# Feature interaction in fp32: pairs transposed and weighed eight at a time in two shared PSUM banks, with the two steps two sets of scores apart

## What is computed

```
bilinear = einsum('bie,ied->bid', feature, weight)
out      = einsum('bid,bjd->bij', bilinear, feature)
```

## Time and profile before

| | |
|---|---|
| time, median of 3 runs | 1518.4 us (1517.48 to 1518.64) |
| the profiled execution | 1516.77 us, its span 1514.9 us |
| TensorE matmul busy | 1452.9 us, 96% |
| VectorE busy | 1167.2 us, 77% |
| ScalarE busy | 893.5 us, 59% |
| DMA traffic | 438.67 MB, mean 290 GB/s |

### The profile page before, as it was taken

How to read it: one execution, slowest core, us unless ns; L and a number is a source line. 1 busy time by engine, 2 the same in 40 slices (tenths; PEclk the granted TensorE clock), 3 DMA queues, 4 the chain that set the end, 5 groups by cost and what they waited for, 6 DMA issues and landing times.

```text
span 1514.9 us, 41346 instructions
## 1 busy us (share of the span) xinstructions
PE 1452.9 (96%) x16192; PEld 1206.3 (80%) x16192; DVE 1167.2 (77%) x2048; ACT 893.5 (59%) x1313; POOL 294.3 (19%) x518
## 2 busy tenths in 40 slices
PE   7999999999999999999999999999999999999965
PEld 6888887888788787888778888788787888878754
DVE  0578778788777778778787787877877777887897
ACT  5665665656656565665656656566665656656532
POOL 0112112121221212122121121221212111121222
PEclk9999999999999999999999999999999999999999
DMA  8799999999999999999999999999999999999898
GB/s 220 225 289 288 305 300 290 299 288 304 300 290 296 294 300 292 303 290 287 290 294 303 294 295 305 292 297 292 296 299 292 301 284 305 298 292 297 265 275 257
DMA packets 308574, 438.67 MB, mean 290 GB/s; under 512 B 56480, under 2 KB 255136, under 8 KB 308384
## 3 DMA queue, kind: packets, MB, share of 16 engines
q1 hardware_dynamic: 283808, 422.80, 87.1%
q0 software_dynamic: 24576, 13.24, 6.0%
HBM read 108.13 MB, written 327.68 MB: 288 GB/s over the span
## 4 chain that ended last, share of the span: by engine, by line
PE 83%; DVE 10%; DMA 3%; issue 3%; SPq 1%; ACT 0%; POOLq 0%
PE ps L225 43%; PE bp L209 24%; PE tp L193 14%; DVE staging L256 4%; DMA x<-feature_dram 3%; DVE win L305 3%; DVE win L312 2%; PE ps L209 1%; DVE win L313 1%; PE ps L193 1%; SPq L143 0%; SPq L138 0%; SPq L131 0%; ACT staging L256 0%; ACT bl L279 0%
## 5 line engine op out<-in xcount | busy, mean ns | idle before, releaser
L225 PE MATMUL ps<-win,bl 64*100 64x200 f32 x8192 | 831.7, 344 | 42.8 <-DVE win L313 39.6
L225 PEld LDWEIGHTS ps<-win,bl 64*100 64x100 f32 x8192 | 696.5, 207 | 134.3 <-issue 67.1
L256 DVE COPY staging<-ps 100x800 f32<-100x800 f32 x512 | 503.9, 984 | 252.2 <-PE ps L225 252.2
L256 ACT COPY staging<-ps 100x800 f32<-100x800 f32 x512 | 423.3, 827 | 251.9 <-PE ps L225 251.9
L176 POOL DMA_DIRECT2D out_dram<-staging x512 | 293.6, 573 | 1213.3 <-DVE staging L256 985.5
L209 PE MATMUL bp<-xt,w 64*64 64x128 f32 x6144 | 419.6, 276 | 0.0
L209 PEld LDWEIGHTS bp<-xt,w 64*64 64x64 f32 x6144 | 326.7, 133 | 65.2 <-issue 65.2
L279 ACT COPY bl<-bp 128x512 f32<-128x512 f32 x384 | 225.2, 586 | 178.0 <-PE bp L209 178.0
L269 ACT COPY xt<-tp 128x512 f32<-128x512 f32 x384 | 225.1, 586 | 171.4 <-PE tp L193 171.4
L305 DVE COPY win<-xt 128x400 f32<-128x400 f32 x512 | 272.9, 533 | 64.5 <-ACT xt L269 48.8
L193 PE MATMUL tp<-ident,x 128*128 128x128 f32 x1536 | 252.9, 287 | 7.9 <-DMA x<-feature_dram 7.6
(11 more groups left out here) (5 smaller groups left out, 0.6 us busy)
## 6 DMA issues: line engine op xcount, KB each, us to landing
out_dram<-staging SPq DMA_DIRECT2D x1024, 300.0 KB, 4.7
x<-feature_dram SPq DMA_DIRECT2D x400, 256.0 KB, 5.1
out_dram<-staging POOLq DMA_DIRECT2D x512, 25.0 KB, 4.6
w<-weight_dram SPq DMA_DIRECT2D x24, 128.0 KB, 3.9
w<-weight_dram SPq DMA_DIRECT2D x2, 64.0 KB, 3.3
```

The costliest lines, as they stand in the source:

```text
L225: last = nc.tensor.matmul(ps[s % TILES][0:FH, h, F * b:F * (b + 1)], rows_of_bl(n, R * k + PB * i + b)[64 * h:64 * h + 64], win[64 * h:64 ...
L256: copy(staging[:, slot, :, :, :].rearrange("p b h j -> p h b j"), ps[s % TILES][0:FH, :, 0:PB * F].rearrange("p h (b j) -> p h b j", j=F)) ...
```

## The change

- A group is now eight pairs (12 groups of eight and one of four, NG = 13), and its `x` comes in one transfer of 512 KB. XSLOTS stays 4, so the slots hold twice as much.
- T makes eight transposes, B sixteen matmuls. Both write into the same two banks, `made`, which take the place of `tp` and `bp`. So a T now also waits for the last B's copy (`bl_stored`), and B for T's copy, as before.
- T and B are no longer next to each other. The places are counted in sets: T of group u after set 4u + 4 + 2(u // 6), and B of it two sets later. B of group 0 comes after set 4, T of the next block's first group after set 62.
- A transpose writes its 128 columns in runs of four numbers, 16 numbers apart, so that the PSUM tile already has the layout of `xt`. Before, the transpose wrote 128 neighbouring numbers and ScalarE's copy read runs of four.
- ScalarE copies a group at once: 1024 numbers per partition in place of two copies of 512.
- Output slots go from 16 to 12, windows from 3 to 4. SyncE issues the load of a group right after the T that frees its slot, four groups ahead.

The diff, cut to its core:

```diff
--- before.py
+++ after.py
-    NG = FH // C
+    LINES = FH // C
+    GROUPS = [8] * (FH // 8) + [FH % 8]
+    NG = len(GROUPS)
...
-    OSLOTS = 16
-    WSLOTS = 3
-    WG = 2
+    OSLOTS = 12
+    WSLOTS = 4
...
-    weighed_at = {t * 7 // 6: t for t in range(NG)}
-    transposed_at = {k: t + 1 for k, t in weighed_at.items() if t + 1 < NG}
-    transposed_at[QUADS - 1] = NG
+    transposed_at = {4 * u + 4 + 2 * (u // 6): u for u in range(1, NG)}
+    weighed_at = {s + 2: u for s, u in transposed_at.items()}
+    weighed_at[4] = 0
+    transposed_at[SETS_B - 2] = NG
...
-        x = sbuf("x", [128, XSLOTS, 2 * C * E])
+        x = sbuf("x", [128, XSLOTS, 16 * E])
...
-        tp = ctx.enter_context(nc.psum_tensor("tp", [128, 512], F32))
-        bp = ctx.enter_context(nc.psum_tensor("bp", [128, 512], F32))
+        made = ctx.enter_context(nc.psum_tensor("made", [128, 2, 512], F32))
...
-        def transpose_tile(n, t):
-            return tp_first[t % 3] if n == 0 else tp[:]
-
-        def bilinear_tile(n, t):
-            return bp_first[t % 3] if n == 0 else bp[:]
+        def transpose_tile(n, u):
+
+            tile = ps[0] if n == 0 and u % 2 else made
+            cells = tile[:].rearrange("p l (k c r) -> p l k c r", c=C, r=R)
+            return cells[:, 0:GROUPS[u] // C]
+
+        def bilinear_tile(n, u):
+            return ps[1 + u % 2] if n == 0 else made
...
-            for t in range(NG + XSLOTS):
-                if t % WG == 0 and t < NG:
-                    load_w(t // WG)
-                load_x(t)
+            for u in range(NG + 1 + XSLOTS):
+                if u < NG:
+                    load_w(u)
+                load_x(u)
             for n in range(BLOCKS):
-                for k in range(QUADS):
-                    store(n * SETS_B + 2 * k)
-                    store(n * SETS_B + 2 * k + 1)
-                    if k in transposed_at:
-                        at = (n + 1) * NG + transposed_at[k] + XSLOTS - 1
+                for s in range(SETS_B):
+                    store(n * SETS_B + s)
+                    if s in transposed_at:
+                        at = (n + 1) * NG + transposed_at[s] + XSLOTS
...
             def transposes(at):
...
                 if n:
                     pe.wait_ge(xt_stored, at)
-                elif t >= 3:
-                    pe.wait_ge(xt_stored, t - 2)
-                for c in range(C):
-                    last = nc.tensor.transpose(transpose_tile(n, t)[:, NB * c:NB * (c + 1)],
+                    pe.wait_ge(bl_stored, at)
+                elif u >= 2:
+                    pe.wait_ge(xt_stored, u - 1)
+                for c in range(GROUPS[u]):
+                    last = nc.tensor.transpose(transpose_tile(n, u)[:, c // C, :, c % C, :],
                                                x[:, at % XSLOTS, 2 * E * c:2 * E * (c + 1)], ident[:])
...
-                for k in range(QUADS):
-                    scores(n, k, 0)
-                    scores(n, k, 1)
-                    if k in transposed_at and (n + 1) * NG + transposed_at[k] < BLOCKS * NG:
-                        transposes((n + 1) * NG + transposed_at[k])
-                    if k in weighed_at and n + 1 < BLOCKS:
-                        bilinear(n + 1, weighed_at[k])
+                for s in range(SETS_B):
+                    scores(n, s // 2, s % 2)
+                    if s in transposed_at and (n + 1) * NG + transposed_at[s] < BLOCKS * NG:
+                        transposes((n + 1) * NG + transposed_at[s])
+                    if s in weighed_at and n + 1 < BLOCKS:
+                        bilinear(n + 1, weighed_at[s])
...
-                nc.scalar.copy(group_of_xt(n, t),
-                               transpose_tile(n, t).rearrange("p (c k r) -> p k c r", c=C, r=R)
+                nc.scalar.copy(group_of_xt(n, u), transpose_tile(n, u).rearrange("p l k c r -> p k l (c r)")
                                ).then_inc(xt_stored, 1)
...
-                nc.scalar.copy(group_of_bl(n, t), bilinear_tile(n, t).rearrange(cells, c=C)
-                               ).then_inc(bl_stored, 1)
+                rows = bilinear_tile(n, u)[:].rearrange("p a c -> p (a c)")[:, 0:NB * GROUPS[u]]
+                nc.scalar.copy(group_of_bl(n, u), rows.rearrange(cells, b=NB)).then_inc(bl_stored, 1)
```

More of the change, by code:

```diff
@@ L36, in feature_interaction @@
     TILES = 3
-    OSLOTS = 16
-    WSLOTS = 3
-    WG = 2
+    OSLOTS = 12
+    WSLOTS = 4
     FA = FH // 16 * 16
-    assert 2 * E == 128 and B % NB == 0 and FH % C == 0 and NG <= QUADS and R == 2 * PB
-    assert PB * F <= 512 and C * NB == 512 and OSLOTS % 2 == 0 and (BLOCKS * SETS_B) % OSLOTS == 0
+    assert 2 * E == 128 and B % NB == 0 and FH % 8 == C and R == 2 * PB
+    assert PB * F <= 512 and OSLOTS % 2 == 0
     feature_v = feature.rearrange("b f e -> b (f e)")
@@ L46, in feature_interaction @@
     out_v = out.rearrange("b (m h) j -> m b (h j)", h=2)
-    weighed_at = {t * 7 // 6: t for t in range(NG)}
-    transposed_at = {k: t + 1 for k, t in weighed_at.items() if t + 1 < NG}
-    transposed_at[QUADS - 1] = NG
-    assert len(weighed_at) == NG and max(weighed_at) < QUADS - 2 and all(k >= t for k, t in weighed_at.items())
+    transposed_at = {4 * u + 4 + 2 * (u // 6): u for u in range(1, NG)}
+    weighed_at = {s + 2: u for s, u in transposed_at.items()}
+    weighed_at[4] = 0
+    transposed_at[SETS_B - 2] = NG
+    assert all(s >= 2 * min(2 * u + 1, LINES - 1) + 1 for s, u in weighed_at.items())
     ctx = ExitStack()
@@ L96, in feature_interaction, with line_of_xt, group_of_xt, group_of_bl @@
         block = ctx.enter_context(nc.Block())
-        def transpose_tile(n, t):
-            return tp_first[t % 3] if n == 0 else tp[:]
-        def bilinear_tile(n, t):
-            return bp_first[t % 3] if n == 0 else bp[:]
-        def group_of_xt(n, t):
-            return xt[:, t, :, :, :] if n % 2 == 0 else xt[:, :, t, :, :]
+        def transpose_tile(n, u):
[4 more added lines that the diff above has]
+            return ps[1 + u % 2] if n == 0 else made
+        def line_of_xt(n, t):
+            return xt[:, t, :, :, :] if n % 2 == 0 else xt[:, :, t, :, :]
+        def group_of_xt(n, u):
+            lines = slice(2 * u, 2 * u + GROUPS[u] // C)
+            if n % 2 == 0:
+                return xt[:, lines].rearrange("p l k c r -> p k l (c r)")
+            return xt[:, :, lines].rearrange("p k l c r -> p k l (c r)")
         def quad_of_xt(n, k):
-            return xt[:, 0:NG, k, :, :] if n % 2 == 0 else xt[:, k, 0:NG, :, :]
-        def group_of_bl(n, t):
+            return xt[:, 0:LINES, k, :, :] if n % 2 == 0 else xt[:, k, 0:LINES, :, :]
+        def group_of_bl(n, u):
             if n % 2 == 0:
-                return bl[:, C * t:C * (t + 1), :]
-            return bl[:, :, C * t:C * (t + 1)]
+                return bl[:, 8 * u:8 * u + GROUPS[u], :]
+            return bl[:, :, 8 * u:8 * u + GROUPS[u]]
         def rows_of_bl(n, b):
@@ L234, in _ @@
             transposes(1)
[L235 to L238, removed]
+            for u in range(NG):
+                bilinear(0, u)
+                if u + 2 < NG:
+                    transposes(u + 2)
             transposes(NG)
             for n in range(BLOCKS):
-                for k in range(QUADS):
-                    scores(n, k, 0)
-                    scores(n, k, 1)
-                    if k in transposed_at and (n + 1) * NG + transposed_at[k] < BLOCKS * NG:
-                        transposes((n + 1) * NG + transposed_at[k])
-                    if k in weighed_at and n + 1 < BLOCKS:
-                        bilinear(n + 1, weighed_at[k])
+                for s in range(SETS_B):
[4 more added lines that the diff above has]
+                        bilinear(n + 1, weighed_at[s])
         def stage(engine, copy, staged, s):
@@ L262, in store_xt @@
             def store_xt(at):
-                n, t = at // NG, at % NG
+                n, u = at // NG, at % NG
                 act.wait_ge(transposed, at + 1)
+                lines = GROUPS[u] // C
                 if n:
                     act.wait_ge(bilinear_done, n * NG)
-                    act.wait_ge(own_filled, (n - 1) * QUADS + t + 1)
-                nc.scalar.copy(group_of_xt(n, t),
-                               transpose_tile(n, t).rearrange("p (c k r) -> p k c r", c=C, r=R)
+                    act.wait_ge(own_filled, (n - 1) * QUADS + 2 * u + lines)
@@ L288, in _ @@
             store_xt(NG)
             for n in range(BLOCKS):
-                for k in range(QUADS):
-                    stage(act, nc.scalar.copy, staged_act, n * SETS_B + 2 * k)
-                    if k in transposed_at and (n + 1) * NG + transposed_at[k] < BLOCKS * NG:
-                        store_xt((n + 1) * NG + transposed_at[k])
-                    if k in weighed_at and n + 1 < BLOCKS:
-                        store_bl(n + 1, weighed_at[k])
+                for s in range(SETS_B):
+                    if s % 2 == 0:
```

(5 more changed lines are left out.)

53 lines of the change are left out of this document (26 added, 27 removed).

## The result

| | before | after |
|---|---|---|
| median | 1517.9 us (1515.8 to 1518.6, 4 runs) | 1465.1 us (1464.6 to 1466.7, 4 runs) |
| ratio, 95% interval | | 0.9656 [0.9639, 0.9673] |
| profiled execution | 1516.8 us | 1466.7 us |
| its span | 1514.9 us | 1464.8 us |
| the scores begin at | 51.55 us | 53.46 us |

The change makes the kernel 3.4% faster. The forecast was 1451 us with a range of 1436 to 1492. The two profiled executions lie 50.1 us apart and the medians 52.8 us. The sum had said 67.5.

The account below looks back on a forecast made before the run. TensorE's own list was taken to set the pace of the 15 mixed blocks. 53.1 + 10.5 + 2 + 1.9 = 67.5 us off 1516.8 gave 1449.3; with 1.6 us for the median, 1451 us, range 1436 to 1492.

Parts of the forecast that it names:

- Fewer bursts: TensorE, 15 mixed blocks: 12 fewer bursts each of T and B save 3.54 us a block, 53.1 us in all.
- New neighbours: TensorE: T now followed by scores and B preceded by them; extra price 0 to 0.12 us, taken as 0.
- The rival of 0.12 us: Scores behind a T are dearer by 0.12 us, 23 us over 15 blocks: 1474 us; chance 0.12.
- The shared banks: T and B wait for each other's ScalarE copy, 1.01 us for 1024 numbers, covered by two sets: cost nothing.
- late copies: Rival: ScalarE's two-bank copy takes 1.6 us or is queued, T and B wait some 0.1 us each: 1490 us; chance 0.04.
- The end of a block: VectorE's stall falls from 2.0 us to 1.2 (even) or up to 1.5 (odd): 0.7 us less a block, 10.5 in all.
- the ledger: Count of VectorE's copies from set 59's start: set 57's copy ended at -0.64, rounds end at 4.32, 6.61 and 8.90 us.
- Opening: Before the scores: 12 fewer bursts of each kind save 3.5 us, larger first transfers cost some; 2 us less taken.
- `x` transfers: Loads issued four groups ahead, some 24 us in place of 9, so the 1.9 us of waits for `x` go.
- The DMA rival: Mixed blocks ask for 308 GB/s; if the DMA engines give 300, a block takes 90.1 us: 1486 us; chance 0.10.
- The slower rival: Transposes writing PSUM in runs of four with gaps take 0.22 us, not 0.11: 165 us more, 1616 us; chance 0.09.
- The rule on changes of tiling mode: Skill's rule: TensorE pays 0.18 us per mode change, so eight pairs save 0.36, not 0.295 us: 12 us more, 1439 us.

Follow-up runs that it names:

- experiment 2: Kernel before, with T moved between the two sets of a quad, so one more burst of scores a round: 1599.9 us, ratio 1.052.
- Experiment 6: Changed kernel with the two-set gaps at groups 4, 8 and 12 in place of 6 and 12: 1453.2 us, ratio 0.9568 to the kernel before.
- experiment 1: Kernel before, but its transposes write runs of four numbers with gaps, as in the changed kernel: 1516.1 us, ratio 0.9982.
- experiment 4: Kernel before with four windows in place of three and 12 output slots in place of 16: 1517.5 us, ratio 1.0004.
- Experiment 12: Changed kernel loading only the first group's weights and using them in every group: 1459.7 us, ratio 0.9601 to the kernel before.
- experiment 3: Changed kernel with three windows in place of four: 1568.4 us, ratio 1.0322 to the kernel before.
- experiment 7: Changed kernel with ScalarE, not VectorE, staging sets 57, 61 and 1 of each block: 1459.1 us, ratio 0.9612 to the kernel before.
- experiment 9: Kernel of experiment 7 with 14 output slots in place of 12 and three `x` slots in place of four: 1462.7 us, ratio 0.964.
- experiment 8: Kernel of experiment 7, loading only half of each group's `x` from block 1 on, all computing kept: 1437.3 us, ratio 0.948.
- experiment 10: Kernel of experiment 6, with ScalarE staging one in four of the last block's odd sets: 1455.5 us, ratio 0.9595 to the kernel before.

## Why the prediction was right, and where its sum was off

**Fewer bursts.** Forecast 53.1 us. T took 1.02 us for a forecast of 1.03 and B 1.89 for 1.90, with 12 bursts less of each in a block. This term stands, and experiment 2 confirms that a burst has a fixed price by adding one of scores (80 us expected, 82 measured).

**New neighbours.** Taken as free, and so they were. T followed by scores took no more than T followed by B. The rival of 0.12 us falls, and the longer time in the earlier trace rows was VectorE's window, as argued.

**The shared banks.** ScalarE's copy of 1024 numbers took 1.01 us, as worked out, and no T or B of the mixed blocks waited for it. One T did, at the end of the opening, where it stands right behind the last B: 0.82 us, once. The forecast had not seen that wait. In the mixed blocks late copies are no cause.

**The end of a block.** This is the step that failed: 10.5 us of gain forecast. A mean block became 92.0 - 88.7 = 3.3 us shorter, where 3.54 + 0.7 = 4.24 was forecast. That is 0.9 us a block, 14 us in all. The new stall is 1.9 us in an even and 2.4 us in an odd block, where the ledger had 1.2 and up to 1.5. The old end had cost 2.0 and 2.3. So the end of a block gave nothing back. Of the 0.9 us this is 0.7, and two runs of four sets that cost about 0.1 us more each are the other 0.2. The ledger began VectorE at rest: it put the end of set 57's copy 0.64 us before set 59. VectorE's timeline shows otherwise:

```profile
665.77 0.97 DVE L266 COPY staging<-ps 100x800 f32<-100x800 f32 x1
...
668.04 0.98 DVE L266 COPY staging<-ps 100x800 f32<-100x800 f32 x1
...
677.23 0.97 DVE L266 COPY staging<-ps 100x800 f32<-100x800 f32 x1
```

The second of these is set 57's copy. It ends at 669.02, 0.17 us after set 59 began (668.85) and 0.8 us later than in the ledger. Ahead of it stand sets 53 to 56 in a row, and the T and B after them have only four pairs, so VectorE had been at work without a pause since set 53's copy.

Not all of the 0.8 us reach TensorE. The third copy is that of set 1, for which set 4 waits. It ends at 678.20, 9.35 us after set 59 began, where the ledger had 8.90, so 0.45 us arrive. The rest of the 0.8 us between 1.93 and 1.15 is that set 4 starts 0.15 us behind the copy and then takes 0.85 us, where the ledger had 0 and 0.69. Experiment 6 takes two sets out of that stretch and gains 6 to 10 us in these blocks, but as said there its size can't tell a backlog from a ledger begun at rest. The backlog is read from the timelines, and no run took it away alone.

**Opening.** Forecast 2 us of gain, measured 1.9 us of loss, so 3.9 us. Together the two terms make 18 us, which is what lies between 67.5 and 50.1. Part of the second is this execution's. The five other traces of the new opening begin the scores at 50.74 to 51.59 us, and those of the old opening in experiments 1, 2 and 4 at 50.37 to 50.69. By these the loss is some 0.6 us and the error 2.6, and the medians lie 52.8 us apart. There is no gain either way. The working allowed for one late transfer at the beginning, and took the rest to be TensorE's. The DMA engines then had 0.79 MB to bring for each T and B of 2.9 us, 271 GB/s, and managed 239 here and 251 to 271 in the others. Experiment 12 shows it.

**`x` transfers and what was taken as nothing.** The waits for `x` went, as forecast. But the fourth window, of which I said only that it leaves VectorE's copies as they are, is worth 103 us in the new order (experiment 3), and nothing in the old one with four slots for `x` (experiment 4). I had counted its help at the block's end and not its part in the regular rounds.

**The DMA rival.** It had 0.10 and did not come true at 308 GB/s: there is no wait for a transfer in the mixed blocks of the changed kernel. It was close. The versions that took most of the stall off VectorE ran into it (experiments 7 and 9), and experiment 8 shows that it was this and nothing on the computing side. The kernel of experiment 6 stands at the edge: its trace has such waits, and that of experiment 10, with the same mixed blocks, has none.

**The slower rival.** It is refuted by experiment 1. The page of the Trainium skill that speaks for it (SBUF — State Buffer, Door 1: The DMA port swizzle) is not borne out for runs of four fp32 numbers written by a transpose. The rule on changes of tiling mode (TensorEngine Tiling (Array Packing), Key Properties) would have given 0.36 us for eight pairs. In the trace two rounds of four pairs took 6.50 us and one round of eight takes 6.19, in an odd block 6.28 and 5.99. That is 0.31 and 0.29, and the price list said 0.295. In experiment 2 that rule's 0.18 us for each change of mode would give 375 x 0.18 = 68 us, where the price of the scores' own bursts gave 80, and 82 were measured. In these kernels each new burst is also a change of mode, so the runs speak against one price for all changes, and not against the drain as its cause.

**What stays open.** Why four sets in a row take 0.12 us more than before. VectorE's copy of set 53 ends some 0.26 us before set 56 should start, and the trace puts down no wait.

## What to carry to other kernels

Count the bursts in which an engine does one kind of work. If beginning one has a fixed price, double the work in each, and take the price from two bursts of different length in the trace. When you place such bursts, follow every other engine through the whole cycle, because a backlog is made earlier than where the wait shows, and a buffer more that gains nothing in the old order may carry the new one. Before relieving the engine that is waited for, compare the rate of data that the new pace asks for with what the DMA engines reach when they are all busy.

## What was not expected of the hardware

In the changed kernel single windows of 5 us reached this rate, above the 333 GB/s in the kernel before:

```profile
805.00:810.00 5.00, 5.00 (x65) 4.48 (x65) 4.12 (x9) 2.97 (x4) 1.14 (x2) 1.00 1.03 365
```

It is above the 358 GB/s or so that the Trainium skill, DMA: Bandwidth & Descriptors, Specifications, gives for a core. The same page of the Trainium skill says under Bandwidth that this is each core's half when both cores of a pair stream, and here the kernel runs on one core. From 93 to 1380 us no version went beyond 307 GB/s, with the engines 97 to 98% busy. In the opening, with weights in pieces of 256 bytes among the data, the same engines gave 239 to 271. That the pieces are the reason is not shown: without the weights the engines were not all busy (68%).
